# Norm in front of the attention: the value products are issued between the transposes of the norm instead of behind them

## What is computed

```python
x = x + _layernorm(_L0_ffn_ref(_layernorm(x), ...))
h = _layernorm(x)
q, k, v = h @ Wq.T + bq, h @ Wk.T + bk, h @ Wv.T + bv     # 32 heads of 16
scores = einsum('bhqd,bhkd->bhqk', q, k) / sqrt(16)        # causal, then softmax
out = softmax(scores) @ v
```

## Time and profile before

| | us |
|---|---|
| median of 3 runs | 1784.63 |
| lowest and highest | 1781.35, 1789.15 |
| the profiled execution | 1799.58 |
| its span, first to last instruction | 1797.8 |
| PE busy | 1571.5 (87%) |
| DVE, POOL, ACT busy | 1229.0, 942.2, 828.4 |
| mean granted TensorE clock | 0.938 of full speed |

### The profile page before, as it was taken

How to read it: one execution, slowest core, us unless ns; L and a number is a source line. 1 busy time by engine, 2 the same in 40 slices (tenths; PEclk the granted TensorE clock), 3 DMA queues, 4 the chain that set the end, 5 groups by cost and what they waited for, 6 DMA issues and landing times.

```text
span 1797.8 us, 26599 instructions
## 1 busy us (share of the span) xinstructions
PE 1571.5 (87%) x8870; PEld 1235.1 (69%) x8870; DVE 1229.0 (68%) x2024; ACT 828.4 (46%) x1639; POOL 942.2 (52%) x861
## 2 busy tenths in 40 slices
PE   3789999999989999999999759995689999988791
PEld 2567877877878777778787547884456776766581
DVE  5577777778778777787787765556547766768525
ACT  2355554544544544555544323332047666664131
POOL 3257567576566675765766643004334423427454
PEclk9899999999999999999999879998789999998796
DMA  3102011011021110110211012231000000041334
GB/s 113 36 15 87 19 48 59 12 47 60 15 70 37 44 58 18 47 60 14 83 31 46 14 59 73 69 114 36 0 1 13 13 1 1 1 165 71 110 137 164
DMA packets 49497, 92.60 MB, mean 52 GB/s; under 512 B 8016, under 2 KB 32720, under 8 KB 44176
## 3 DMA queue, kind: packets, MB, share of 16 engines
q1 hardware_dynamic: 45744, 79.58, 13.8%
q0 software_dynamic: 3680, 12.06, 2.0%
HBM read 81.14 MB, written 10.49 MB: 51 GB/s over the span
## 4 chain that ended last, share of the span: by engine, by line
PE 61%; DVE 16%; POOL 8%; issue 7%; ACT 4%; DMA 3%; SPq 1%; another core or an unknown queue 0%; POOLq 0%; ACTq 0%; DVEq 0%
PE banks L355 30%; PE banks L1717 6%; PE banks L1836 3%; PE banks L1641 3%; PE banks L1635 3%; PE banks L1727 2%; PE banks L1795 2%; POOL wol L360 2%; DMA x<-in_w_gate 2%; DVE tap L1195 2%; PE banks L1826 2%; PE banks L1650 2%; DVE xbc L1201 2%; DVE acc L623 2%; PE banks L1609 2%
## 5 line engine op out<-in xcount | busy, mean ns | idle before, releaser
L1195 DVE SCALAR_TENSOR_TENSOR tap<-banks,parg,tap 128x511 f32<-128x511 f32 (+2 forms) x288 | 215.1, 747 | 41.3 <-ACT tap L922 33.9
L705 POOL TENSOR_TENSOR am<-ah,upto 128x1024 fp32r<-128x1024 f32 x64 | 124.3, 1942 | 216.3 <-PE banks L1609 201.3
L857 POOL TENSOR_SCALAR kz<-kst,head 128x512 fp32r<-128x512 f32 x64 | 99.1, 1567 | 160.2 <-DVE kst L1413 160.2
L355 PE MATMUL banks<-xTh,wch 128*128 128x512 f32 x384 | 163.5, 426 | 8.1 <-DVE em L1299 7.8
L355 PE MATMUL banks<-xTh,wcl 128*128 128x512 f32 x384 | 151.3, 394 | 0.0
L355 PE MATMUL banks<-xTl,wch 128*128 128x512 f32 x384 | 151.1, 393 | 0.0
L1127 ACT ACTIVATE prob<-banks,nmax 128x128 f32<-128x128 f32 (+3 forms) x256 | 121.8, 530 | 53.9 <-DVE nmax L1429 53.8
L930 ACT ACTIVATE th<-tap 128x512 f32<-128x512 f32 x96 | 60.6, 631 | 171.2 <-DVE tap L1195 169.1
L1429 DVE TENSOR_REDUCE nmax<-banks 128x2 f32<-128x256 f32 (+3 forms) x128 | 104.9, 819 | 39.9 <-PE banks L1827 39.7
L705 POOL TENSOR_TENSOR am<-al,upto 128x1024 fp32r<-128x1024 f32 x64 | 123.7, 1932 | 0.0
L922 ACT ACTIVATE tap<-banks,parg 128x512 f32<-128x512 f32 x96 | 74.6, 777 | 92.3 <-PE banks L355 91.2
(11 more groups left out here) (289 smaller groups left out, 4492.5 us busy)
## 6 DMA issues: line engine op xcount, KB each, us to landing
x<-grownT SPq DMA_DIRECT2D x96, 128.0 KB, 4.8
x<-in_w_conv SPq DMA_DIRECT2D x7, 1536.0 KB, 6.7
x<-in_w_gate SPq DMA_DIRECT2D x8, 1024.0 KB, 5.1
x<-in_w_out SPq DMA_DIRECT2D x8, 1024.0 KB, 4.8
eraw<-in_expert_w SPq DMA_DIRECT2D x8, 1024.0 KB, 7.2
gur<-in_ff_gu SPq DMA_DIRECT2D x7, 1024.0 KB, 4.8
x<-in_hidden SPq DMA_DIRECT2D x16, 256.0 KB, 4.1
mates<-yd SPq DMA_DIRECT2D x8, 512.0 KB, 4.3
```

The costliest lines, as they stand in the source:

```text
L355: m = nc.tensor.matmul(o, a, b, start=first and n == 0, stop=last and n == len(terms) - 1)
L705: m = pool.tensor_tensor(am[:, part, :, :], a[:, i, :].bitcast(F32).unsqueeze(2).to_broadcast([P, HG, P]), upto[:, :].unsqueeze(1).to_broa ...
L857: m = pool.tensor_scalar(kz[:, quad % 2, p2, j, :], kst[:, p2, :].bitcast(F32), head[:, j:j + 1], None, ALU.mult)
L1195: nc.vector.scalar_tensor_tensor(tap[:, q % 2, sh:L], bk(CONV_BANKS[q % 2])[:, 0:L - sh], parg[:, KC * q + k:KC * q + k + 1], tap[:, q % 2 ...
```

## The change

On PE, each tile's transposes are still issued in the old order, but behind those of tile i now come the 12 matmuls of the value product of tile i-2, into bank 2 or 3; the last two products stand alone behind the last transposes. Value product i waits for `lo` of its own tile, and from the third on for the evacuation of the one two before. The wait for `lo` of all tiles goes, waits for aw_lo and hid_f stand ahead of the norm. On DVE, the evacuation of value product n-6 is issued between norm round n and the remainder (`norm_low`) that follows it, for n = 6 to 11, the last two behind the norm. DVE's wait for the small loads (the bias) goes ahead of the norm. ACT, POOL and SP keep their instructions and their order.

```diff
-        def norm_vector(q, start=0):
+        def norm_vector(q, start=0, after=None):
             lag, made = 4 if q else 2, 0
             for n in range(start, NT + lag):
                 norm_round(q, n)
+                if after:
+                    after(n)
                 while q < STAGES and made <= n - lag and made < (NT if n == NT + lag - 1 else 2 * (n - start) + 2):
                     norm_low(q, made)
                     made += 1
...
+        def norm_turn(q, i):
+            norm_wait(nc.tensor, q, "xn", i + 1)
+            if i >= 2:
+                norm_wait(nc.tensor, q, "lo", i - 1)
+            for k in range(KT):
+                mmi = nc.tensor.transpose(bk(i % 2)[:, k * P:(k + 1) * P], acc[:, i, k * P:(k + 1) * P], ident[:, :])
+            mmi.then_inc(nsem["tr"], 1)
+
         def norm_tensor(q):
             for i in range(NT):
-                norm_wait(nc.tensor, q, "xn", i + 1)
...
+                norm_turn(q, i)
...
                 add_down(FP - 1, 1)
-                norm_vector(2)
+                dve.wait_ge(small_in, 16 * 13)
+
+                def values(i):
+
+                    dve.wait_ge(v_ps, i + 1)
+                    nc.vector.tensor_tensor(v[:, i, 0:AH * VW].rearrange("p (h d) -> p h d", h=AH)[:, :, 0:HD],
+                                            bk(2 + i % 2).rearrange("p (h d) -> p h d", h=AH),
+                                            abv[:, :].rearrange("p (h d) -> p h d", h=AH), ALU.add).then_inc(v_f, 1)
+
+                norm_vector(2, 0, lambda n: values(n - 6) if n >= 6 else None)
+                for i in range(NT - 2, NT):
+                    values(i)
             if STAGES >= 3:
-
-                dve.wait_ge(small_in, 16 * 13)
...
-                for i in range(NT):
-                    dve.wait_ge(v_ps, i + 1)
-                    nc.vector.tensor_tensor(v[:, i, 0:AH * VW].rearrange("p (h d) -> p h d", h=AH)[:, :, 0:HD],
-                                            bk(i % 2).rearrange("p (h d) -> p h d", h=AH),
-                                            abv[:, :].rearrange("p (h d) -> p h d", h=AH), ALU.add).then_inc(v_f, 1)
...
             if STAGES >= 3:
-                norm_tensor(2)
-                norm_wait(pe, 2, "lo", NT)
+                def values(i):
+
+                    norm_wait(pe, 2, "lo", i + 1)
+                    if i >= 2:
+                        pe.wait_ge(v_f, i - 1)
+                    tok = slice(i * P, (i + 1) * P)
+                    products(bk(2 + i % 2), [(xTh[:, k, tok], xTl[:, k, tok], awh[:, k, :], awl[:, k, :])
+                                             for k in range(KT)]).then_inc(v_ps, 1)
+
                 pe.wait_ge(aw_lo, KT)
+                pe.wait_ge(hid_f, 4 * FP)
+                for i in range(NT + 2):
+                    if i < NT:
+                        norm_turn(2, i)
+                    if i >= 2:
+                        values(i - 2)
...
-                for i in range(NT):
-                    if i >= 2:
-                        pe.wait_ge(v_f, i - 1)
-                    tok = slice(i * P, (i + 1) * P)
-                    products(bk(i % 2), [(xTh[:, k, tok], xTl[:, k, tok], awh[:, k, :], awl[:, k, :])
-                                         for k in range(KT)]).then_inc(v_ps, 1)
                 pe.wait_ge(sel_ready, SEL)
```

## The result

| | before | after |
|---|---|---|
| median, 7 runs each | 1784.63 us | 1772.44 us |
| lowest and highest | 1780.79, 1793.55 | 1766.84, 1779.16 |
| ratio after/before, 95% interval | | 0.9934 (0.9908 to 0.9960) |
| the profiled execution | 1799.58 us | 1772.24 us |
| its span | 1797.8 us | 1770.5 us |

The kernel became 0.66% faster (0.40 to 0.92%); 1770.3 us and 0.80% had been forecast. The last line is the stage that the change touches, read from the traces: from the start of tile 0's transposes (1253.13 before, 1240.37 after) to the start of the first projection (1305.73 and 1278.48). It is 14.5 us shorter.

What follows compares the result with a forecast made beforehand. Bound: two stages in sequence, the norm on DVE and POOL, then value products on PE, delaying the first projection. Starting products earlier brings it 14.3 us forward: 1784.63 - 14.3 = 1770.3 us, range 1764.5 to 1779.

Steps and rivals of the forecast that it cites:

- The start of the products: Value products on PE: the first starts 0.85 us behind the start of tile 2's transposes, 18.1 us earlier.
- The prices: Value products on PE: 5.12 us each at the low clock, 2.80 at the high, plus 0.49 for a tile's transposes.
- The clock: PE's clock rises 4.7 us into the value products, so product 0 has 11 matmuls low and one high.
- two trains: Earlier 512-column matmuls on PE that began low: clock rose 3.8 us into value products, 5.6 into feed-forward products.
- rival 3: PE's clock never rises before the projections: 1792.2 us, 0.4% slower; chance 0.04.
- the ring: DVE and POOL waiting for each other in the norm, 4.68 or 3.83 us a round; product 0's wait adds 1.0.
- the walk: PE's path tile by tile from the first product to the first projection, idling 0.4 and 0.6 us.
- rival 1: DVE's in-order queue holds the norm, normed tile 5 at 1277.4 instead of 1275.9: gain 12.8, 1771.8 us; chance 0.09.
- Rival 2: PE's clock stays low through two products and a third of the next: gain 11.3, 1773.3 us; chance 0.10.
- The end: First projection on PE at 1291.45 instead of 1305.73, 14.3 us earlier, 29 us behind tile 2's transposes.
- Rival 4: Loop over heads starts no earlier, or lost time comes back later: 1784.6 us; chance 0.05 together with unseen causes.

Runs made afterwards that it cites:

- six banks: Changed kernel with products in banks 2 to 7 in turn and all eight DVE evacuations behind the norm: stage 37.05 us, ratio 0.9928.
- the run with added matmuls: Changed kernel plus eight unused 512-column matmuls behind the transposes of tiles 0 and 1 each: stage 37.15 us, ratio 0.9926.
- the run with added transposes: Changed kernel plus 16 unused 128-column transposes behind the transposes of tiles 0 and 1 each: stage 37.12 us, run once, no ratio.
- the second measurement: The changed kernel, unaltered, measured again against 17 runs of the kernel before: stage 38.19 us, ratio 0.9906.
- one tile behind: Changed kernel with value product i behind the transposes of tile i+1, evacuated behind its round's remainder: stage 34.84 us, ratio 0.9913 to the kernel before.

## Why the prediction was right

**The start of the products.** Forecast 0.85 us behind the start of tile 2's transposes, measured 0.77.

**The prices.** A product at the low level: forecast 5.12 us, measured 5.20 (1250.40 to 1255.60). At the high level a tile's product with its transposes: forecast 0.49 + 2.80, measured 3.24. The split was a little off: four transposes take 0.35 us (1255.60 to 1255.95) and the first matmul behind them 0.32 instead of 0.23.

**The clock.** I took 4.7 us, midway between two trains; it rose 4.8 us after the first product matmul. The size was luck. It was 4.8 us in all three executions with the same work of PE ahead of the train (the changed kernel twice, six banks once), but 1.9, 2.7 (twice), 3.6 and 3.8 where the train began elsewhere, and nothing in the rows of the kernel before told which. Each microsecond of error is worth 0.45 us of product 0 (0.427 against 0.233 a matmul), of which less than half reached the end of this stage (1.0 of 2.3 us in the run with added matmuls). The reason that I gave for rival 3, that transposes alone leave the level low, was wrong in general: 24 in a row raised it. So was the fear behind it. The Trainium skill's statement that the full rate does not engage for transposes (TensorE: Matmul & The Clock Gate, on PE-mode transpose) is not what the run with added transposes shows. Its case of a clock that oscillates with PSUM banks (section A second HAM failure mode: psum-queue depth-cycling) did not come up, even with 1.28 us of idling between two products.

**DVE and the ring.** Forecast: the wait for product 0 costs the ring 1.0 us; measured 1.1. Forecast waits of PE ahead of tiles 4 and 5: 0.4 and 0.6. The profile shows 0.24 and 0.41; counted as in the walk, from where the next matmul could have started, they are 0.40 and 0.57. Then there are none, as forecast. From evacuation 1 on they are hidden: DVE's idle time in a round shrank by the length of one, and the round kept its length. No idle time of DVE for PE but the first was forecast; evacuations 3 and later have some, with PE setting the end by then. The run with six banks prices all of it at 1.1 us, so rival 1 was wrong. Rival 2, products 0 and 1 at the low level, did not occur in any run. Rival 3's bound was a little off by its own sum: with six low products the first projection would still have come 1.8 us earlier than before, with seven 0.6 later.

**The end.** From tile 2's transposes to the first projection: forecast 28.96 us, measured 28.85, against 43.24 before. The gain of 14.4 us was forecast as 14.3. Nothing was given back: before and after, the first projection stands 17.2 us ahead of the first scores and 492 us ahead of the end. Rival 4 is out by that.

**From the stage to the device time.** 12.2 us by the medians, 7.1 to 16.4 by the interval, 12 to 22 by that of the second measurement: the 14.4 of the trace lies in both. The profiled executions are 27.3 us apart, and 12.8 of that is ahead of the stage. The forecast left this open (the execution stood 15 us above the median). It is in the state space layer, which the change doesn't touch: 14.0 us in the stretch below, less 1.2 us the other way outside it. The same stretch between two weight loads, in windows of the kernel before and of the changed one:

```profile
250.40:649.30 398.90, 378.53 (x2047) 305.49 (x2046) 309.41 (x445) 200.11 (x388) 265.06 (x225) 0.97 0.15 44
```

```profile
251.10:636.00 384.90, 372.79 (x2047) 301.08 (x2046) 300.14 (x445) 199.97 (x388) 264.81 (x225) 0.99 0.16 46
```

Equal instruction counts, 14.0 us apart, at a granted clock of 0.97 and 0.99. PE's busy time explains 5.7 us of it. Of the rest, 6.9 us is one wait of PE, seven times for the remainder ynTl that DVE makes (L360): 12.4 us in the first trace, 5.5 in the second. What makes one execution differ from the other there stays open. Carrying the gain over to the median as a difference, and not as the difference of two profiled executions, was what kept this out of the forecast.

## What to carry to other kernels

Where one stage idles the engine that the next stage needs, issue the next stage's work per tile behind the tile that it depends on, in buffers that the running stage does not use, and read the new length as a walk: start of the stream, sum of its work, waits for the slower engine. An earlier start is worth somewhat less than its size, because transposes, waits and more time at the low level join the stream (14.5 of 18.3 us here), and it is worth something only as long as the moved stream sets the end; at one tile behind it was the norm's own ring again, and warming PE or freeing DVE brought nothing more. An evacuation that waits in an in-order queue needs its place checked against both ends: the bank it frees and the work that it stands behind.

## What the runs showed of the hardware

- Transposes raised TensorE's clock from its 1.2 to its 2.4 GHz level: 24 f32 transposes in a row (5.2 us) did, in the one execution that had them; eight at a time with 0.64 us between did not the earlier trace rows.
- The same products, entered at the low level, needed between 1.9 and 4.8 us until the clock rose, depending on the kernel: product 0 took 3.8 us in the one and 5.2 in the other.
- A short wait of PE costs more than the idle time that the profile shows: 0.65 us of idling in two places stretched two tiles by 0.98 us.
